# Reordering the load queue behind the context loop of a perceiver block

## Chip, cores, metric

One core of one Trainium2 chip. The metric is the device time in microseconds of one execution of the whole kernel, as the median of several runs. The profiled execution is one more run.

## What is computed

`x` is 256 x 2048, the context 25088 x 2048. Cut to what matters:

```python
def reference(x, ctx, Wq, bq, Wk, bk, Wv, bv, W_base, b_base, W_gate, A, B):
    x = x + cross_attention(layernorm(x), ctx)        # softmax(q @ ctx.T) @ ctx, no projections
    h = layernorm(x)                                  # 32 heads of 64, 8 of them for k and v
    q = einsum('bse,edh->bsdh', h, Wq) + bq           # Wq is summed over groups of 4 heads first
    k = einsum('bse,edh->bsdh', h, Wk) + bk
    v = einsum('bse,edh->bsdh', h, Wv) + bv
    # for each token: scores over the 64 x 64 pairs of head *elements*, softmax, times v
    x = x + attention_within_token(q, k, v)
    h = layernorm(x)
    result = h @ W_base.T + b_base
    probs = softmax(h @ W_gate.T); top-2 of 8 experts, renormalised -> route_w
    delta = einsum(einsum(h, A) * route_w, B)         # LoRA experts of rank 16
    return x + result + delta
```

## The kernel before, in words

The kernel is written engine by engine, and each engine runs its own list in order; semaphores tie them together. The order of the loads is the order in which the SP list issues them. Every float32 product is made of three float32r products, of a high half (`nat_hi`, `xt_hi`) and a low half (`nat_lo`, `xt_lo`), the latter being the difference to the former (L1004 to L1006).

**The loop.** 49 blocks of 512 context rows. A block comes twice: as quarters (`quart`, L330), which VectorE transposes into chunks for the scores, and as rows in four pieces of 1 MB (`raw`, L323), which ScalarE casts to `nat_hi` (`hi_piece`, L557) and GpSimd subtracts to `nat_lo` (`lo_piece`, L475). `raw` holds two pieces: piece j + 2 can be loaded once piece j has been split, which is what `nat_ready[j]` counts. Wq's sum over head groups is made in the loop and stored to `wq_dram`.

**Behind the loop** three weights are read in the same four pieces, in the order Wk, Wq (from `wq_dram`), Wv. SP's list before: two pieces of Wk; bk and bv (L398); eight loads of LoRA's B into `b_nat` (L401), each 16 x 128 rows of 64 B; four loads of the gate into `side_rows` and four of LoRA's A into `a_nat` (L338), rows of 128 B; then the other ten pieces in a list `order` with the waits on `nat_ready`. Within the list stand `store_qk(0, 1)` (L415), which stores k to DRAM in three bfloat16 parts when VectorE has counted `qk_split`, and `heads_back(1, k_t, ...)` (L423), twelve loads that bring the parts back with tokens along the free axis; each has eight rows of 16 KB. Behind the list come q's store and q's twelve loads into `q_t`, then `b_base_all` (L438), and, when TensorE has done the gate (`G_GATE`), the second half of the first block of W_base (L330). `b_nat` and `side_rows` lie in the buffer that this half takes.

**ScalarE** casts Wk piece 0, makes `std` of the first tile of tokens (L540), casts piece 1, drains that tile's transposes into `xt_hi`, casts pieces 2 and 3, and then makes `std` of the second tile. **GpSimd** splits Wk, **VectorE** splits Wq and Wv (L881) and the parts of q and k (L887, L893).

**TensorE** multiplies the first tile of 128 tokens by all of Wk, transposes the second tile, multiplies that one; then Wq for both, then Wv for both, with the bias as a product ahead of each (L1120). Then it waits for `b_loaded` and `a_loaded`, transposes B and A in groups of four (L1034, L1013) and the gate (L1155), waits for `qk_back`, and starts the attention scores (`pair_scores`, L1165). Attention, the third layer norm, the router and the base product follow. The lines in its list around this place:

```python
            pe.wait_ge(b_loaded, 16 * EXPERTS)
            pe.wait_ge(a_loaded, 16 * QR)
            ...
            pe.wait_ge(qk_back, 16 * TT * (len(Q_PARTS) + len(K_PARTS)))
            ...
            for o in range(2):
                pair_scores(o)
```

Of the kernel before, what the change touches and what calls it, by code (L numbers as in the profile page):

```python
# [14 lines left out]
P = 128  # L15
# [13 lines left out]
def perceiver_block(nc, x, ctx, wq, bq, wk, bk, wv, bv, w_base, b_base, w_gate, lora_a, lora_b, out):  # L29
# [9 lines left out]


    _, TOK, DIM = x.shape
    KEYS = ctx.shape[1]
    DH, HEADS = bq.shape
    KVH = bk.shape[1]
    REP = HEADS // KVH
    EXPERTS, RANK, _ = lora_a.shape
    OUTF = w_base.shape[0]
    TT = TOK // P
    DC = DIM // P
    KB = 512  # L50
    KT = KB // P
    NB = KEYS // KB
# [8 lines left out]
    QR = P // SQ  # L61
# [24 lines left out]
    with ExitStack() as stack:  # L86
        def sem(name):
            return stack.enter_context(nc.semaphore(name))
# [10 lines left out]
        def put(at, name, shape, dt=F32):  # L99
            return nc.alloc_sbuf_tensor_at(name, shape, dt, offset=at)  # L100
# [21 lines left out]
        a_nat = put(at_tr, "a_nat", [P, DIM])  # L122
# [22 lines left out]
        k_t = put(at_probs, "k_t", [P, P, DH], BF16)  # L145
        x_hat2 = put(at_probs, "x_hat2", [P, TT, DIM])
        side_rows = put(at_quart + 16 * KIB, "side_rows", [P, DIM])
        b_nat = put(at_quart + 24 * KIB, "b_nat", [P, DC, ER])
# [76 lines left out]
        chunk_split = sem("chunk_split")  # L225
# [25 lines left out]
        a_loaded = sem("a_loaded")  # L251
        b_loaded = sem("b_loaded")
        gate_loaded = sem("gate_loaded")
# [67 lines left out]
        def _(sp):  # L321
            def load_rows(j, src):
                sp.dma_start(raw[:, j % 2], src).then_inc(raw_loaded[j], 16)  # L323
# [12 lines left out]
            def load_in_chunks(to, src, a, done):  # L336

                sp.dma_start(to.rearrange("p (c a i) -> p a c i", a=QR, i=SQ)[:, a],  # L338
                             src[:, a * QF:(a + 1) * QF].rearrange("p (c i) -> p c i", i=SQ)).then_inc(done, 16)
# [57 lines left out]
            for col, b_ in enumerate((bk, bv)):  # L397
                sp.dma_start(side_rows[0:1, col * QKC:(col + 1) * QKC],  # L398
                             b_.rearrange("(a d) h -> a (d h)", a=1)).then_inc(bias_loaded, 16)
            for e in range(EXPERTS):  # L400
                sp.dma_start(b_nat[:, :, e * RANK:(e + 1) * RANK],  # L401
                             lora_b[e].rearrange("(o p) r -> p o r", p=P)).then_inc(b_loaded, 16)
            for a in range(QR):
                load_in_chunks(side_rows[64:64 + EXPERTS, :], w_gate, a, gate_loaded)
            sp.wait_ge(chunk_split, DC * NB)
            for a in range(QR):
                load_in_chunks(a_nat[:], lora_a.rearrange("e r d -> (e r) d"), a, a_loaded)
            sp.wait_ge(wq_stored, 16 * DC)


# [1 line left out]
            def store_qk(n, w):  # L412
                for t in range(TT):
                    sp.wait_ge(qk_split, TT * n + t + 1)
                    sp.dma_start(qk_dram[w, :, :, t * P:(t + 1) * P].rearrange("s g m d -> m (s g) d"),  # L415
                                 qk_nat[:, w, t].rearrange("p s (g d) -> p (s g) d", d=DH)).then_inc(qk_stored, 16)

            def heads_back(w, to, parts):
                sp.wait_ge(qk_stored, TT * (2 - w) * 16)
                for k, part in enumerate(parts):  # L420
                    for t in range(TT):
                        at = P // TT * t + KVH * k
                        sp.dma_start(to[at:at + KVH], qk_dram[w, part, :, t * P:(t + 1) * P]).then_inc(qk_back, 16)  # L423

            order = [(n, src, j) for n, src in enumerate((wk_rows, wq_rows, wv_rows)) for j in range(PIECES)]
            for n, src, j in order[2:]:
                if (n, j) == (2, 1):
                    store_qk(0, 1)
                if (n, j) == (2, 2):
                    heads_back(1, k_t, K_PARTS)  # L430
                sp.wait_ge(nat_ready[(j + 2) % 4], NB + n + (j >= 2))
                load_rows(j, src[:, 4 * j:4 * j + 4, :])
            store_qk(1, 0)
            for j in range(PIECES):
                sp.wait_ge(nat_ready[j], NB + 3)
            heads_back(0, q_t, Q_PARTS)
            sp.wait_ge(qkv_done, 3 * TT)
            sp.dma_start(b_base_all[:], b_base.unsqueeze(0).broadcast_to([P, OUTF])).then_inc(bias_loaded, 16)  # L438

# [800 lines left out]
K_PARTS = (0, 1, 0, 1, 2, 0)  # L1240
# [24 lines left out]
```

## Time and profile before

| | us |
|---|---|
| median of 3 runs | 2553.24 |
| lowest, highest | 2550.48, 2562.08 |
| profiled execution | 2560.45 |
| its span from first to last instruction | 2558.6 |
| TensorE busy in the span | 2458.9 (96%) |
| VectorE busy | 1975.5 (77%) |
| GpSimd busy | 1265.1 (49%) |
| ScalarE busy | 1081.6 (42%) |

All times of instructions below are counted from the start of the span. A line such as `start us, us, engine line op out<-in xcount [idle before <-releaser]` tells when an instruction began, how long it took, and, in brackets, how long the engine had been idle before it and whose event ended that. For a transfer the time is that of the issue on the SP queue; the time to its landing stands in the DMA view. The loop ends near 2198 us; the stretch that the change touches reaches from there to the start of attention.

### The profile page before, as it was taken

How to read it: one execution, taken by the hardware profiler on the slowest of the kernel's cores; microseconds unless marked ns; L12 is line 12 of the kernel's file. 1: busy time of each engine (PE TensorE's matmuls, PEld its weight loads, DVE VectorE, ACT ScalarE, POOL GpSimd, SP SyncE). 2: the span in 40 equal slices, each digit the busy share in tenths (PEclk: the TensorE clock that was granted, in tenths of full speed). 3: DMA queues.
4: the chain of work that ended last, by engine and by line, in shares of the span. 5: the costliest groups of instructions: out<-in, count | busy, mean ns of one | idle time of the engine just before them, and what ended most of it. 6: DMA issues, size and time to landing. Idle time of an engine off the chain costs nothing.

```text
span 2558.6 us, 35034 instructions
## 1 busy us (share of the span) xinstructions
PE 2458.9 (96%) x11342; PEld 2025.2 (79%) x11342; DVE 1975.5 (77%) x2668; ACT 1081.6 (42%) x1547; POOL 1265.1 (49%) x896
## 2 busy tenths in 40 slices
PE   6999999999999999999999999999999999894799
PEld 4888888888888888888888888888888888763677
DVE  7788888888888888888888887787878778532668
ACT  4444444444444444444444444444444444222323
POOL 4455556565556556655665565555555555410000
PEclk9999999999999999999999999999999999996579
DMA  9787887788788778878887877787777777667046
GB/s 243 200 217 182 215 202 195 200 209 212 194 206 213 195 196 209 206 197 213 201 204 194 210 190 189 191 196 184 192 184 186 188 188 192 166 138 113 5 85 145
DMA packets 377515, 476.14 MB, mean 186 GB/s; under 512 B 48707, under 2 KB 265795, under 8 KB 374853
## 3 DMA queue, kind: packets, MB, share of 16 engines
q1 hardware_dynamic: 373894, 454.68, 73.3%
q0 software_dynamic: 3584, 20.97, 2.6%
q8 instruction: 23, 0.38, 0.1%
q14 instruction: 14, 0.11, 0.0%
HBM read 467.74 MB, written 7.86 MB: 186 GB/s over the span
## 4 chain that ended last, share of the span: by engine, by line
PE 89%; DMA 4%; DVE 3%; SPq 2%; ACT 1%; POOL 1%; issue 1%; DVEq 0%; ACTq 0%
PE ps L1004 28%; PE ps L1006 28%; PE ps L1005 28%; PE ps L1013 2%; DMA raw<-in_L_attn_Wv_dram 1%; DMA q_t<-qk_dram 1%; DVE ch_lo L768 1%; PE ps L1034 1%; SPq L330 1%; DMA raw<-in_ctx_dram 1%; POOL nat_lo L475 1%; PE ps L1197 1%; DVE tr L764 1%; ACT nat_hi L557 1%; PE ps L1165 0%
## 5 line engine op out<-in xcount | busy, mean ns | idle before, releaser
L475 POOL TENSOR_TENSOR nat_lo<-raw,nat_hi 128x512 fp32r<-128x512 f32 x800 | 1172.8, 1496 | 933.3 <-ACT nat_hi L557 931.0
L768 DVE TENSOR_TENSOR ch_lo<-tr,ch_hi 128x512 fp32r<-128x512 f32 x848 | 949.9, 1120 | 362.6 <-ACT ch_hi L534 360.7
L534 ACT CAST ch_hi<-tr 128x512 fp32r<-128x512 f32 x848 | 517.2, 621 | 876.2 <-PE ps L1006 857.1
L1004 PE MATMUL ps<-ch_hi,xt_hi 128*128 128x512 f32 x1696 | 674.5, 398 | 8.1 <-DVE ch_lo L768 7.7
L1006 PE MATMUL ps<-ch_hi,xt_lo 128*128 128x512 f32 x1696 | 663.5, 391 | 0.0
L1005 PE MATMUL ps<-ch_lo,xt_hi 128*128 128x512 f32 x1696 | 662.9, 391 | 0.0
L1004 PE MATMUL ps<-nat_hi,pt_hi 128*128 128x512 f32 x1568 | 610.3, 389 | 2.9 <-DVE pt_lo L698 2.9
L1006 PE MATMUL ps<-nat_hi,pt_lo 128*128 128x512 f32 x1568 | 610.2, 389 | 0.0
L1005 PE MATMUL ps<-nat_lo,pt_hi 128*128 128x512 f32 x1568 | 610.0, 389 | 0.0
L764 DVE STREAM_TRANSPOSE tr<-quart 128x512 f32<-128x512 f32 x848 | 592.8, 699 | 3.9 <-DMA quart<-in_L_ffn_W_base_dram 3.8
L557 ACT CAST nat_hi<-raw 128x2048 fp32r<-128x2048 f32 x208 | 397.5, 1911 | 276.9 <-PE ps L1006 215.3
L1004 PEld LDWEIGHTS ps<-ch_hi,xt_hi 128*128 128x128 f32 x1696 | 320.0, 189 | 77.5 <-DVE ch_lo L768 9.1
L1006 PEld LDWEIGHTS ps<-ch_hi,xt_lo 128*128 128x128 f32 x1696 | 319.7, 189 | 68.4
L1005 PEld LDWEIGHTS ps<-ch_lo,xt_hi 128*128 128x128 f32 x1696 | 320.0, 189 | 64.4 <-issue 0.8
L1004 PEld LDWEIGHTS ps<-nat_hi,pt_hi 128*128 128x128 f32 x1568 | 294.3, 188 | 65.3 <-DVE pt_lo L698 4.0
L1005 PEld LDWEIGHTS ps<-nat_lo,pt_hi 128*128 128x128 f32 x1568 | 294.3, 188 | 61.3
L1006 PEld LDWEIGHTS ps<-nat_hi,pt_lo 128*128 128x128 f32 x1568 | 294.3, 188 | 61.2
L806 DVE SCALAR_TENSOR_TENSOR acc<-acc,alpha,ps 128x512 f32<-128x512 f32 x248 | 177.6, 717 | 41.9 <-PE ps L1006 40.2
L518 ACT CAST pt_hi<-ps 128x512 fp32r<-128x512 f32 x98 | 57.2, 584 | 120.8 <-PE ps L1013 120.8
L815 DVE SCALAR_TENSOR_TENSOR acc<-acc,alpha,ps 128x512 f32<-128x512 f32 x144 | 101.2, 703 | 4.9 <-PE ps L1006 4.9
L563 ACT ACTIVATE probs<-ps,neg_max 128x512 f32<-128x512 f32 x98 | 66.9, 683 | 67.4 <-DVE neg_max L788 67.4
L785 DVE TENSOR_REDUCE blk_max<-ps 128x1 f32<-128x512 f32 x98 | 65.5, 668 | 6.8 <-PE ps L1006 6.8
(126 smaller groups left out, 941.7 us busy)
## 6 DMA issues: line engine op xcount, KB each, us to landing
quart<-in_ctx_dram SPq DMA_DIRECT2D x392, 512.0 KB, 8.3
raw<-in_ctx_dram SPq DMA_DIRECT2D x196, 1024.0 KB, 7.8
wq_in<-in_L_attn_Wq_dram POOLq DMA_DIRECT2D x16, 1024.0 KB, 11.9
quart<-in_L_ffn_W_base_dram SPq DMA_DIRECT2D x32, 512.0 KB, 8.6
wq_dram<-wq_out POOLq DMA_DIRECT2D x16, 256.0 KB, 2.3
raw<-in_L_attn_Wk_dram SPq DMA_DIRECT2D x4, 1024.0 KB, 6.3
raw<-wq_dram SPq DMA_DIRECT2D x4, 1024.0 KB, 5.2
raw<-in_L_attn_Wv_dram SPq DMA_DIRECT2D x4, 1024.0 KB, 17.6
```

The source lines that it names most:

```text
L475: last = pool.tensor_tensor(nat_lo[:, j, t], raw[:, j % 2, t], nat_hi[:, j, t].bitcast(F32), ALU.subtract)
L534: act.copy(ch_hi[:, c % RING_CH, :], tr[:, c % RING_TR, :]).then_inc(chunk_hi, 1)
L557: act.copy(nat_hi[:, j], raw[:, j % 2]).then_inc(nat_hi_ready, 1)
L563: act.activation(probs[:, q, :], ps[:, SCORE_BANK + TT * new + q, :], ACT.Exp, bias=neg_max[:, new, q:q + 1], accum_out=row_sum[:, q:q + 1 ...
L764: dve.transpose(tr[:, c % RING_TR, :].rearrange("p (r i) -> p r i", i=SQ), src).then_inc(chunk_transposed, 1)
L768: dve.tensor_tensor(ch_lo[:, c % RING_CH, :], tr[:, c % RING_TR, :], ch_hi[:, c % RING_CH, :].bitcast(F32), ALU.subtract).then_inc(chunk_s ...
L785: dve.tensor_reduce(blk_max[:, q:q + 1], ps[:, SCORE_BANK + TT * new + q, :], AX.X, ALU.max, negate=True).then_inc(blkmax_ready, 1)
L806: dve.scalar_tensor_tensor(piece, piece, alpha[:, 1 - turn.parity, q:q + 1], ps[:, out_bank(v, turn.over), :], ALU.mult, ALU.add).then_inc ...
L815: dve.scalar_tensor_tensor(piece, piece, alpha[:, turn.parity, q:q + 1], ps[:, out_bank(v, False), :], ALU.mult, ALU.add).then_inc(acc_upd ...
L1004: pe.matmul(out_, a_hi, b_hi, start=start, stop=False)
L1005: pe.matmul(out_, a_hi, b_lo, start=False, stop=False)
L1006: return pe.matmul(out_, a_lo, b_hi, start=False, stop=stop)
```

## The change

SP's list behind the loop is put in another order. No transfer is added, removed or changed in shape, and no other engine's list is touched.
- The eight B loads, the four gate loads and the four A loads (with the wait on `chunk_split` ahead of the latter) go from behind bk and bv to behind q's way back, ahead of the wait for `qkv_done` and of `b_base_all`.
- The ten other pieces of Wk, Wq and Wv follow bk and bv at once.
- k's store goes from ahead of Wv's second piece to behind Wq's last, ahead of Wv's first. k's way back is now written behind the load of Wv's second piece, where before it was written ahead of the wait for Wv's third.

```diff
             for col, b_ in enumerate((bk, bv)):
                 sp.dma_start(side_rows[...], b_...).then_inc(bias_loaded, 16)
+            sp.wait_ge(wq_stored, 16 * DC)
...
+            order = [(n, src, j) for n, src in enumerate((wk_rows, wq_rows, wv_rows)) for j in range(PIECES)]
+            for n, src, j in order[2:]:
+                sp.wait_ge(nat_ready[(j + 2) % 4], NB + n + (j >= 2))
+                load_rows(j, src[:, 4 * j:4 * j + 4, :])
+                if (n, j) == (1, 3):
+                    store_qk(0, 1)
+                if (n, j) == (2, 1):
+                    heads_back(1, k_t, K_PARTS)
+            store_qk(1, 0)
+            for j in range(PIECES):
+                sp.wait_ge(nat_ready[j], NB + 3)
+            heads_back(0, q_t, Q_PARTS)
             for e in range(EXPERTS):
                 sp.dma_start(b_nat[...], lora_b[e]...).then_inc(b_loaded, 16)
             for a in range(QR):
                 load_in_chunks(side_rows[64:64 + EXPERTS, :], w_gate, a, gate_loaded)
             sp.wait_ge(chunk_split, DC * NB)
             for a in range(QR):
                 load_in_chunks(a_nat[:], lora_a..., a, a_loaded)
-            sp.wait_ge(wq_stored, 16 * DC)
...
-            for n, src, j in order[2:]:
-                if (n, j) == (2, 1):
-                    store_qk(0, 1)
-                if (n, j) == (2, 2):
-                    heads_back(1, k_t, K_PARTS)
-                sp.wait_ge(nat_ready[(j + 2) % 4], NB + n + (j >= 2))
-                load_rows(j, src[:, 4 * j:4 * j + 4, :])
-            store_qk(1, 0)
-            for j in range(PIECES):
-                sp.wait_ge(nat_ready[j], NB + 3)
-            heads_back(0, q_t, Q_PARTS)
             sp.wait_ge(qkv_done, 3 * TT)
             sp.dma_start(b_base_all[:], ...).then_inc(bias_loaded, 16)
```

## Rows read from the trace of the kernel before

**Rows 1.** The page, its first line.

```profile
span 2558.6 us, 35034 instructions
```

**Rows 2.** TensorE's waits, 2228 to 2370 us: who waited for whom, sum, times, longest.

```profile
PE ps L1004 <- DVE nat_lo L881: 17.0, 1, 17.0
PE ps L1165 <- DMA q_t<-qk_dram: 16.2, 1, 16.2
PE ps L1004 <- POOL nat_lo L475: 8.7, 2, 8.2
```

**Rows 3.** The chain that ended last, 2050 to 2560 us: start, us, what.

```profile
2293.14 26.55 DMA raw<-in_L_attn_Wv_dram
...
2336.00 21.52 DMA q_t<-qk_dram
...
2426.91 6.17 PE ps L1013 x28
```

**Rows 4.** Timeline of the SP queue: start, time over which issued, line, transfer, count.

```profile
2199.96 7.17 SPq L323 DMA_DIRECT2D raw<-in_L_attn_Wk_dram  x2
...
2207.88 12.75 SPq L401 DMA_DIRECT2D b_nat<-in_L_ffn_B_dram  x8
...
2222.70 6.75 SPq L338 DMA_DIRECT2D a_nat<-in_L_ffn_A_dram  x4
2229.56 2.26 SPq L323 DMA_DIRECT2D raw<-in_L_attn_Wk_dram  x2
...
2272.74 0.37 SPq L323 DMA_DIRECT2D raw<-in_L_attn_Wv_dram  x1
2277.98 2.17 SPq L415 DMA_DIRECT2D qk_dram<-qk_nat  x2
2280.19 1.86 SPq L323 DMA_DIRECT2D raw<-in_L_attn_Wv_dram  x1
2284.43 4.01 SPq L423 DMA_DIRECT2D k_t<-qk_dram  x12
2288.49 5.05 SPq L323 DMA_DIRECT2D raw<-in_L_attn_Wv_dram  x2
...
2332.01 4.29 SPq L423 DMA_DIRECT2D q_t<-qk_dram  x12
```

**Rows 5.** Timeline of GpSimd, 2190 to 2330 us.

```profile
2216.70 10.94 POOL L475 TENSOR_TENSOR nat_lo<-raw,nat_hi 128x512 fp32r<-128x512 f32 x8 [9.96 <-ACT nat_hi L557]
2238.46 10.85 POOL L475 TENSOR_TENSOR nat_lo<-raw,nat_hi 128x512 fp32r<-128x512 f32 x8 [10.82 <-ACT nat_hi L557]
```

**Rows 6.** DMA view, issues in 2200 to 2207 us: count, KB, us to landing.

```profile
raw<-in_L_attn_Wk_dram SPq DMA_DIRECT2D x2, 1024.0 KB, 5.7
```

**Rows 7.** Timeline of ScalarE, 2235 to 2242 us.

```profile
2236.48 1.90 ACT L557 CAST nat_hi<-raw 128x2048 fp32r<-128x2048 f32 x1 [10.53 <-DMA raw<-in_L_attn_Wk_dram]
```

**Rows 8.** DMA view, 2223 to 2233.2 us: packets, and a pair of loads.

```profile
DMA packets 8586, 1.24 MB, mean 122 GB/s; under 512 B 8514, under 2 KB 8514, under 8 KB 8585
...
raw<-in_L_attn_Wk_dram SPq DMA_DIRECT2D x2, 1024.0 KB, 7.4
```

**Rows 9.** DMA view, 2314.2 to 2319 us: packets, MB, share of 16 engines.

```profile
q1 hardware_dynamic: 474, 0.94, 50.6%
```

**Rows 10.** DMA view, issues in 2284 to 2290 us.

```profile
raw<-in_L_attn_Wv_dram SPq DMA_DIRECT2D x1, 1024.0 KB, 28.7
```

**Rows 11.** Tile b_nat: count, ns min/median/max, first and last start.

```profile
L1034 PE MATMUL ps<-ident,b_nat x16: 272/273/332, 2335.1 to 2338.9; 128*128 128x128 f32 x16
```

**Rows 12.** Windows: busy time by engine, granted TensorE clock, DMA share, GB/s.

```profile
2334.00:2342.00 8.00, 6.33 (x54) 5.28 (x52) 4.32 (x7) 5.35 (x11) 2.68 (x3) 1.00 0.81 107
2426.00:2434.00 8.00, 6.59 (x32) 6.35 (x32) 6.54 (x9) 4.42 (x8) 0.00 (x0) 0.57 0.00 0
```

**Rows 13.** DMA view, 2211 to 2223 us: packets.

```profile
DMA packets 16906, 1.27 MB, mean 106 GB/s; under 512 B 16816, under 2 KB 16816, under 8 KB 16906
```

**Rows 14.** Line 330, 2340 to 2359 us: count, ns min/median/max, first and last start.

```profile
L330 SPq DMA_DIRECT2D quart<-in_L_ffn_W_base_dram x4: 334/3493/9389, 2341.5 to 2351.8; - x4
```

More of the change, by code:

```diff
@@ L399, in _ @@
                              b_.rearrange("(a d) h -> a (d h)", a=1)).then_inc(bias_loaded, 16)
[L400 to L407, printed above, removed]
             sp.wait_ge(wq_stored, 16 * DC)
@@ L436, in _ @@
             heads_back(0, q_t, Q_PARTS)
+            for e in range(EXPERTS):
+                sp.dma_start(b_nat[:, :, e * RANK:(e + 1) * RANK],
+                             lora_b[e].rearrange("(o p) r -> p o r", p=P)).then_inc(b_loaded, 16)
+            for a in range(QR):
+                load_in_chunks(side_rows[64:64 + EXPERTS, :], w_gate, a, gate_loaded)
+            sp.wait_ge(chunk_split, DC * NB)
+            for a in range(QR):
+                load_in_chunks(a_nat[:], lora_a.rearrange("e r d -> (e r) d"), a, a_loaded)
             sp.wait_ge(qkv_done, 3 * TT)
```

## Prediction

> **What bounds the kernel now.** I read the page first: its span is 2558.6 us, and the profiled execution took 2560.45 us, against a median of 2553.24 us [rows 1]. Nearly all of it is the loop over the context, in which nothing changes. So I work only on the stretch behind the loop, from 2199.96 us on, when the rows of Wk begin to load, to 2357.5 us, when attention begins. I read the stretch as a chain of waits. TensorE's own waits there are three: 8.7 us for the low halves of Wk that GpSimd makes, 17.0 us for the low halves of Wv, and 16.2 us for q_t on its way back from DRAM [rows 2]. The chain names the two late ends of these: the last Wv load, with 26.55 us from its issue, and q_t, with 21.52 us from its last issue [rows 3]. The reader should see that this stretch hangs on the SP queue and on the transfers behind it, and that from 2357.5 us on everything follows from the start of the attention scores: a step that moves this start moves the end by as much.
>
> **Wk, third and fourth piece: what is removed from ahead of them.** Before, SP issues bk and bv, then eight loads of b_nat (12.75 us), four of the gate and four of a_nat (6.75 us), and only then, at 2229.56 us, the third piece of Wk [rows 4]. What it has to wait for is `nat_ready[0]`, GpSimd's split of piece 0. GpSimd does pieces 0 and 1 as eight instructions from 2216.70 us in 10.94 us [rows 5], so piece 0 is done after half of that, at 2222.2, and piece 1 at 2227.6. In the changed kernel SP stands at exactly these waits. A Wk load that ran with nothing beside it landed 5.7 us after its issue [rows 6]: the third piece lands at 2227.9, the fourth at 2233.4. ScalarE cast the third at 2236.48 [rows 7] and takes 1.9 us, so now the casts end at 2229.8 and 2235.3. GpSimd follows with 5.4 us for each and ends at 2240.8, where it ended at 2238.46 + 10.85 = 2249.3 [rows 5]. That is **8.5 us earlier**. If the loads land in 7.4 us, as a pair did beside other traffic [rows 8], it is 6.8. ScalarE's `std` of the second tile of tokens is queued behind the fourth cast and comes early with it. TensorE has its other half of the first tile done by then, and the second tile, then Wq, follow without a new wait. Wq's loads wait for the same kind of event (GpSimd's splits of Wk, VectorE's of Wq) and move along. I take 8.5.
>
> **Key store one place earlier.** I count this on the old clock, before the shift of 8.5. The old order was first Wv piece at 2272.74, store of k at 2277.98 (2.17 us of issue, with its wait for `qk_split`), second Wv piece at 2280.19, k_t back at 2284.43, third and fourth Wv piece at 2288.49 and up to 2293.5 [rows 4]. Queued behind the store's wait is now the first Wv piece: it is issued near 2280.2 instead of 2272.74. Who needs it is TensorE at the end of Wq. 1 MB of such rows moves in about 2.7 us once it runs: 0.94 MB took the 4.8 us from 2314.2 us on at a share of 50.6% of the engines [rows 9], so 2.4 us of all of them; with issue and landing it is the 5.7 us of [rows 6]. The store's rows end near 2283, so the first piece lands at 2287.5 and its split ends at 2291.7. TensorE had Wq done at 2291.4: it costs nothing, by a margin near nought, with cover if it is late of only the 17.0 us wait for the third piece [rows 2]. What does cost is that k_t now queues behind two Wv pieces, not one. It starts 2.7 us later, and the third and fourth Wv piece land behind it: the third took 28.7 us to land beside k_t [rows 10], and it is its landing that TensorE's 17.0 us wait is for. So 2.7 us of the 8.5 go back. Bounds are 0, if k_t starts as before, and 4: k_t's transfers end near 2314 [rows 9], 29.5 us after their first issue [rows 4], where q_t took 25.5, so that much is what other loads beside such a transfer can cost. The k_t issues themselves keep their place between the second and third piece. **Net 5.8 us earlier** for everything up to q_t's store and its way back: its first issue goes from 2332.01 [rows 4] to 2326.2.
>
> **LoRA and gate rows last: what is added behind q_t.** TensorE's program doesn't change: after Wv it waits for `b_loaded` and `a_loaded`, makes 32 transposes and the 16 small ones of the gate, and only then waits for `qk_back` and starts the scores. Before, all of it was done by 2357.5 - 16.2 = 2341.3, in the shadow of q_t. It began near 2335.1 [rows 11], so it took 6.2 us, at a granted clock of 1.00, the 2.4 GHz level [rows 12]. Now the small loads are issued behind q_t's twelve. Two questions decide the price: how long they take, and whether they run beside q_t.
> How long: b_nat, gate and a_nat are 16384 rows of 64 B and 8704 of 128 B. In 2211 to 2233.2 us lie 16816 + 8514 = 25330 packets under 512 B, which are all of them (the few more are those that count a transfer as landed), so 22.2 us at most [rows 8, 13]. I take 21.7, with 21 as the lower end, as SP was held on the second b_nat load till about 2212. Rows count here, not bytes: 2 MB of long rows would move in 5.4 us by the rate above.
> Beside q_t or not: the third Wv piece, issued right behind k_t's last, landed after 28.7 us instead of 5.7 [rows 6, 10]. And of four W_base loads issued behind q_t from 2341.49 on, one held SP for 9.39 us [rows 14]. Each says that what is issued behind twelve such transfers gets through after them, and that SP is held when it issues more. So the small loads take their 21.7 us from q_t's end on. q_t's end is 2357.5 - 2332.0 = 25.5 us after its first issue [rows 3, 4]. I take 1.5 off the sum of the two, as part of the first b_nat load is through by then, and b_base, which ran beside q_t, now comes last.
> The Trainium skill ("DMA: Bandwidth & Descriptors", section "Bandwidth") gives 6.15 us for a load of 1 MB; by it b_nat and a_nat would be an estimated 12.3 us, and the sum some 9 us less. Its loads are of long rows; the trace here shows 22.2 us for 64 and 128 B rows [rows 8, 13].
> TensorE then has idled for some 40 us. During x_hat's transposes, which came behind a wait too, the granted clock was 0.57 on the mean, near the 1.2 GHz level [rows 12]. There 28 of them took 6.17 us, 0.22 us each [rows 3]. So 32 take 7.0 us, the gate's about 2, together **9 us**, all on the path where it had been hidden. If the clock stayed up it would be 6.2.
>
> **Sum.** -5.8 + 21.7 - 1.5 + 9 = +23.4, which I round to +23 us. Attention starts at 2380.5 instead of 2357.5. Behind it b_base and the W_base loads come 23 us later too, but they are needed in x2 and in the second half of the first output block, some 60 and 100 us later. No load is added or removed. On the profiled execution 2560.45 becomes 2583.5; on the median 2553.24 becomes 2576. By the smaller ends of each step (-8.5 + 21 - 4 + 6.2; the 4 is q_t's time beside no other load at all) it is +15, by the larger (-(6.8 - 4) + 22.2 + 9.3) +29: the likeliest case's own range is 2568 to 2582.
>
> **The rivals.**
> **Small loads run beside q_t.** Had SP not been held, the last a_nat is issued 4.3 + 12.75 + 2.0 + 6.75 = 25.8 us after q_t's first issue, lands 5.7 later, and with 9 us of transposes the scores start 40.5 us after 2326.2, at 2366.7: +9, 2562 us. For it: q_t's transfers have eight rows each and load only part of the DMA engines, since in 2314.2 to 2319 us, after k_t, the share was 50.6% while the rest of Wv drained [rows 9]. Against it: that same stretch shows the other part still waiting its turn, and each small load needs all parts. The Trainium skill (same page, "Why a DMA increments its semaphore by 16 and not by 1") has a DMA of eight rows on the eight lowest-numbered of 16 engines, and the trace agrees with the 50.6%; by it the free half helps only half of each small load.
> **Small loads overtake q_t, and it gets faster.** If rows of 64 B pass between q_t's long rows, and a_nat has landed by 16.5 us after q_t's first issue, the transposes end in q_t's shadow and only the gain is left: -5.8, 2547 us. That is the point from which it decides. Against it: the issue alone takes 25.8 us, whatever the transfers do, so it needs an issue that is faster than on [rows 4].
> **It costs more.** The gain shrinks to 2 us since the k store's new place costs TensorE a wait at Wv, and q_t is 4 us slower beside small rows, as k_t was beside Wv: -2 + 4 + 21.7 + 9 = +33, 2586 us. For it: the margin of the first Wv piece is near nought.
>
> **How the numbers follow.** Forecast 0.70, small loads beside q_t 0.13, overtaking 0.05, dearer 0.12. 0.5% is 12.8 us, about what can be told from no change. Forecast and dearer are slower by more: 0.82, and with the upper end of the second case 0.83. Within 0.5%: 0.12. Faster by more than 0.5% only by overtaking at its best, which at -5.8 is itself within 0.5%: of its 0.05 I put 0.02 on faster and 0.03 on the same, so 0.15 the same. The range reaches from 2562, the case beside q_t, to 2585, near the dearer one.
>
> **What would show it.** Third and fourth Wk load issued near 2222 and 2228, GpSimd's last split ending near 2241; q_t's first issue near 2326; one of the first small issues held for over 10 us; a wait of TensorE of about 40 us that ends on a_nat or b_nat, then the transposes at a clock near 0.5, then scores with no wait for q_t. I am wrong if TensorE waits for q_t still, or if the small loads end less than 35 us after q_t's first issue.

## The result, and the profile after

| | median us | runs | range |
|---|---|---|---|
| before | 2553.69 | 8 | 2550.48 to 2562.44 |
| after | 2572.78 | 8 | 2566.65 to 2580.89 |

The ratio is 1.0067, with a 95% interval of 1.0045 to 1.0090: the changed kernel is slower by 17 to 19 us. The profiled execution took 2572.55 us. The ratios of the experiments below are to the runs of the kernel before that were taken beside them, with medians of 2556.83 us (e1 to e4) and 2554.24 us (e5 to e8).

The page of the changed kernel, its first line, which answers [rows 1]:

```profile
span 2570.8 us, 35034 instructions
```

TensorE's waits from 2228 to 2420 us in the changed kernel (who waited for whom, sum, times, longest), which answer [rows 2]:

```profile
PE ps L1034 <- DMA a_nat<-in_L_ffn_A_dram: 42.5, 1, 42.5
PE ps L1004 <- DVE nat_lo L881: 16.5, 1, 16.5
...
PE ps L1004 <- POOL nat_lo L475: 2.9, 1, 2.9
```

The wait for GpSimd's low halves of Wk shrank from 8.7 to 2.9 us. The one for Wv is what it was. The 16.2 us for q_t are gone, and in their place stands a wait of 42.5 us for a_nat. Nothing waits for q_t any more: it has long landed.

The SP queue (start, time over which issued, line, transfer, count), which answers [rows 4]:

```profile
2202.56 7.17 SPq L323 DMA_DIRECT2D raw<-in_L_attn_Wk_dram  x2
...
2224.41 6.26 SPq L323 DMA_DIRECT2D raw<-in_L_attn_Wk_dram  x2
...
2273.92 2.16 SPq L407 DMA_DIRECT2D qk_dram<-qk_nat  x2
2276.12 2.42 SPq L323 DMA_DIRECT2D raw<-in_L_attn_Wv_dram  x2
2280.87 4.16 SPq L415 DMA_DIRECT2D k_t<-qk_dram  x12
2288.32 4.93 SPq L323 DMA_DIRECT2D raw<-in_L_attn_Wv_dram  x2
...
2327.43 4.00 SPq L415 DMA_DIRECT2D q_t<-qk_dram  x12
2331.47 29.51 SPq L430 DMA_DIRECT2D b_nat<-in_L_ffn_B_dram  x8
...
2363.56 5.68 SPq L338 DMA_DIRECT2D a_nat<-in_L_ffn_A_dram  x4
```

The third and fourth Wk piece go out 21.9 us after the first, where it was 29.6. And the eight b_nat loads, which took 12.75 us to issue ahead of Wk, take 29.51 us behind q_t. The chain of the changed kernel shows where (start, us, what), which answers [rows 3]:

```profile
2331.91 21.54 SPq L430
2353.49 1.44 SPq L430
...
2367.82 5.14 DMA a_nat<-in_L_ffn_A_dram
2373.09 1.09 PE ps L1034 x4
...
2379.36 1.12 PE ps L1155 x16
2380.48 0.82 PE ps L1165 x32
```

The second b_nat issue alone is held for 21.54 us, until q_t's rows are through. What the DMA engines moved meanwhile shows in the DMA view, of 2332 to 2334 us and of 2334 to 2352 us:

```profile
DMA packets 1048, 0.20 MB, mean 98 GB/s; under 512 B 1040, under 2 KB 1040, under 8 KB 1040
```

```profile
q1 hardware_dynamic: 128, 1.05, 47.0%
```

Of the 2048 rows of the first b_nat load, 1024 went in the first 2 us. In the 18 us after them the trace has 64 packets of 16 KB, which are q_t's rows, and no row of b_nat; about half of the 16 engines are busy. All of q_t is 96 such packets, of 2.07 us each (median). Eight of them are under way at a time for 23.3 us, and the last ends at 2352.85 us. So half of the engines are free, but half of the first load is left to the engines that q_t keeps busy. Then come the other loads at their usual pace, and a_nat lands; TensorE makes its transposes, and at 2380.48 the scores start. GpSimd's low halves of Wk, which answer [rows 5]:

```profile
2219.29 10.96 POOL L475 TENSOR_TENSOR nat_lo<-raw,nat_hi 128x512 fp32r<-128x512 f32 x8 [9.95 <-ACT nat_hi L557]
2231.40 12.12 POOL L475 TENSOR_TENSOR nat_lo<-raw,nat_hi 128x512 fp32r<-128x512 f32 x8 [1.15 <-ACT nat_hi L557]
```

The loop itself ended 2.6 us later in this execution (Wk's first load at 2202.56 and not 2199.96). From here on, times in a table count from Wk's first load, so that this does not enter.

| us after Wk's first load | before | before, again | after | after, again |
|---|---|---|---|---|
| GpSimd's last split ends | 49.3 | 47.9 | 41.0 | 41.0 |
| k's store issued | 78.0 | 78.2 | 71.4 | 71.3 |
| q_t's first load issued | 132.1 | 131.9 | 124.9 | 125.0 |
| b_nat's first transpose | 135.1 | 135.1 | 170.5 | 169.1 |
| scores start | 157.6 | 158.8 | 177.9 | 175.9 |
| x_hat's first transpose | 227.0 | 228.1 | 246.3 | 244.4 |
| end | 358.6 | 357.6 | 368.2 | 375.5 |

The columns "again" are second profiles of the same two kernels, taken as e9 and e10 below. Attention starts 18.7 us later on the mean of two. The last row shows something else: from x_hat's first transpose to the end it is 131.7, 129.5, 121.9 and 131.1 us, and that has nothing to do with the change (e9 and e10).

### The profile page after: what moved, and what is told of

Its sections match the earlier page's. It is cut to its first block, busy times and chain, and to the rows that moved or that the text cites. A ratio compares the mean times of both kernels' runs of the same rounds, so it can differ in the third digit from the quotient of the medians.

```text
span 2570.8 us, 35034 instructions
## 1 busy us (share of the span) xinstructions
PE 2445.0 (95%) x11342; PEld 2012.1 (78%) x11342; DVE 1976.1 (77%) x2668; ACT 1080.5 (42%) x1547; POOL 1268.5 (49%) x896
## 4 chain that ended last, share of the span: by engine, by line
PE 89%; DVE 3%; DMA 3%; SPq 2%; ACT 1%; POOL 1%; issue 1%; ACTq 0%; DVEq 0%
PE ps L1004 28%; PE ps L1006 28%; PE ps L1005 28%; PE ps L1013 2%; DMA raw<-in_L_attn_Wv_dram 1%; SPq L430 1%; DVE ch_lo L768 1%; PE ps L1034 1%; POOL nat_lo L475 1%; SPq L330 1%; DVE tr L764 1%; DMA raw<-in_ctx_dram 1%; PE ps L1197 1%; ACT nat_hi L557 1%; PE ps L1165 0%
```

## The experiments

My theory after the result: the transposes of B and A had been hidden in TensorE's wait for q_t; now their loads stand behind q_t, so that TensorE waits for them instead. The gain at Wk is real and smaller. Open were three things: whether k's store has a share, why the small loads wait for q_t (the order of SP's queue, or the DMA engines), and what each small load costs.

### e1: the small loads last, k's store at its old place

```diff
-                if (n, j) == (1, 3):
+                if (n, j) == (2, 0):
                     store_qk(0, 1)
```

> The changed kernel with k's store back at its old place, ahead of Wv's second piece; the small loads stay last. Theory (the small loads carry the whole loss, the store's place is worth nothing): attention starts within 2 us of the changed kernel's once the loop's end is taken off, the time is within 3 us of its 2573 us. Rival (the store's new place costs the 2.7 us of the prediction, as k_t queues behind two Wv pieces): q_t's first issue is 2.7 us earlier against the end of Wk's splits than in the changed kernel. The wait of TensorE for a_nat is 42 to 43 us by both.

Measured: 2571.82 us (2569.81 to 2574.96, 5 runs), ratio to before 1.0059 [1.0038, 1.0079]. Its SP queue, first Wk and q_t loads:

```profile
2201.73 7.17 SPq L323 DMA_DIRECT2D raw<-in_L_attn_Wk_dram  x2
...
2327.32 4.00 SPq L415 DMA_DIRECT2D q_t<-qk_dram  x12
```

q_t's first issue is 125.6 us after Wk's first load, 0.7 us later than in the changed kernel and not 2.7 earlier; the wait for a_nat is 41.6 us. As far as these runs can tell, the small loads' place carries the whole loss, and k's store shows no share in it.

### e2 and e11: k's store alone

```diff
-                if (n, j) == (2, 1):
-                    store_qk(0, 1)
...
+                if (n, j) == (1, 3):
+                    store_qk(0, 1)
```

> The kernel before with k's store one place earlier and nothing else; the small loads stand ahead of Wk's third piece again. Theory: no change that can be told, 2552 to 2556 us; Wk's splits end 49 to 50 us after Wk's first load is issued, as before, and TensorE waits some 16 us for q_t. Rival (the earlier store delays k_t and by it Wv's last pieces): q_t's first issue 2.7 us later than before, 2557 us.

Measured: 2554.84 us (11 runs), ratio 1.0004 [0.9989, 1.0020]. In time no difference can be told (the interval reaches from 3 us less to 5 us more). But its profile did not fit: q_t's first issue came 136.2 us after Wk's first load, 4 us later than before.

The SP queue of e2, first Wk and q_t loads:

```profile
2200.95 7.18 SPq L323 DMA_DIRECT2D raw<-in_L_attn_Wk_dram  x2
...
2337.11 4.29 SPq L423 DMA_DIRECT2D q_t<-qk_dram  x12
```

A second profile of the same kernel, e11, was to tell spread from cost:

> The kernel of e2_store_only, profiled once more: there q_t's first issue came 4.1 us later after Wk's first load than in before (136.2 against 132.1), in part since k's store itself came 1.9 us later. Theory (that is the spread of k_t's stretch from execution to execution): 131 to 135 us here. Rival (the store's place costs it): 136 us again.

The same two rows of e11's SP queue:

```profile
2200.47 7.19 SPq L323 DMA_DIRECT2D raw<-in_L_attn_Wk_dram  x2
...
2332.79 4.29 SPq L423 DMA_DIRECT2D q_t<-qk_dram  x12
```

132.3 us, as before. TensorE was late already at k's store in e2 (80.0 us after Wk's first load against 78.1 here). The rest lies in the stretch from k's store to q_t's first issue, and that differs much from execution to execution: with the store at its new place it took 53.5 and 53.7 us (after, e10), 49.5 (e3), 55.4 (e4), 55.2 (e6), 56.2 (e2) and 54.3 (e11), at the old place 54.0, 53.7 (before, e9) and 52.9 us (e1). On the means that is 0.4 us more. The store's place costs nothing that can be told, but a cost of 1 or 2 us could hide in such a spread.

### e3: the small loads on a queue of their own

They are taken out of SP's list and stand in ScalarE's, behind the copies of v_dup.

```diff
-            for e in range(EXPERTS):
-                sp.dma_start(b_nat[...], lora_b[e]...).then_inc(b_loaded, 16)
...
+            act.wait_ge(qk_stored, 4 * 16)
+            act.wait_ge(chunk_transposed, DC * NB)
+            for e in range(EXPERTS):
+                act.dma_start(b_nat[...], lora_b[e]...).then_inc(b_loaded, 16)
...
+            act.wait_ge(chunk_split, DC * NB)
+            for a in range(QR):
+                act_in_chunks(a_nat[:], lora_a..., a, a_loaded)
```

> The changed kernel, but the sixteen small loads are issued by ScalarE's queue in place of SP's, at the same time: behind a wait for q's store and the two v_dup copies, so some 4 us after q_t's first issue. Theory (on SP's queue the second small load stands behind q_t's long rows, because one queue is served in its order): on a queue of their own the small rows go beside q_t, no issue is held for 21 us, and TensorE's wait for a_nat falls from 42.5 us to 20 to 28 us; the time is 2551 to 2560 us. Rival (it is the DMA engines that are busy with q_t, not the queue that is in order): the wait for a_nat stays at 40 to 46 us, the time at 2570 to 2580.

Measured: 2573.58 us (6 runs), ratio 1.0075 [1.0050, 1.0099]. My theory fell. The chain:

```profile
2324.05 21.88 ACTq L639
2345.96 4.33 ACTq L639
```

TensorE's waits in the same kernel:

```profile
PE ps L1041 <- DMA a_nat<-in_L_ffn_A_dram: 45.2, 1, 45.2
```

ScalarE's queue issues its first b_nat load 2.4 us after q_t's first, has the second held for 22.4 us (21.88 of them in the chain), just as SP had, and TensorE waits 45.2 us. (From q_t's first issue to the first transpose it is 47.5 us, against 45.7 and 44.0 in the changed kernel.) The small loads do not wait because they share a queue with q_t. The DMA view of 2328 to 2346 us shows what ScalarE's queue got through:

```profile
q1 hardware_dynamic: 206, 1.56, 71.4%
q10 hardware_dynamic: 104, 0.01, 1.2%
```

Its own queue did let small rows in between q_t's: 104 rows of 64 B, beside 64 rows of 16 KB, where SP's queue had let none. But that is one or two small rows for each long one, and the rest of the load waited. What is left is the DMA engines: each small load has a share on all of them, and those that carry q_t's long rows come to it last. e5 puts that to the test.

### e4: the small loads in gaps of the queue

The edit is shown against the changed kernel; the lines at the small loads' place behind q_t go.

```diff
+            for e in range(EXPERTS):
+                sp.dma_start(b_nat[...], lora_b[e]...).then_inc(b_loaded, 16)
             sp.wait_ge(wq_stored, 16 * DC)
...
+                if (n, j) == (1, 1):
+                    for a in range(QR):
+                        load_in_chunks(side_rows[64:64 + EXPERTS, :], w_gate, a, gate_loaded)
+                    sp.wait_ge(chunk_split, DC * NB)
+                    for a in range(QR):
+                        load_in_chunks(a_nat[:], lora_a..., a, a_loaded)
```

> The changed kernel with no small load last: the eight b_nat loads stand ahead of Wk's third piece, as in the kernel before, the four gate and four a_nat loads behind Wq's second piece, where SP and the DMA engines rest. Theory (the gain of 7 us comes from the a_nat loads that held Wk's third piece back; b_nat alone ends before that piece may be issued): GpSimd's last split ends 8 us earlier than before, attention starts 6 to 8 us earlier than before, the transposes of b_nat and a_nat lie in q_t's shadow again; 2545 to 2549 us. Rival (what is gained at Wk is given back at Wv or to TensorE's clock): attention starts within 3 us of before, 2551 to 2556 us.

Measured: 2553.13 us (2539.51 to 2557.85, 12 runs), ratio 0.9980 [0.9963, 0.9997]. GpSimd's splits of Wk:

```profile
2218.81 10.96 POOL L476 TENSOR_TENSOR nat_lo<-raw,nat_hi 128x512 fp32r<-128x512 f32 x8 [9.95 <-ACT nat_hi L558]
2230.93 12.24 POOL L476 TENSOR_TENSOR nat_lo<-raw,nat_hi 128x512 fp32r<-128x512 f32 x8 [1.15 <-ACT nat_hi L558]
```

TensorE's waits in e4, for q_t and for Wv:

```profile
PE ps L1166 <- DMA q_t<-qk_dram: 17.6, 1, 17.6
PE ps L1005 <- DVE nat_lo L882: 16.8, 1, 16.8
```

The last split ends 41.1 us after Wk's first load, 8.2 less than before, and attention starts at 151.7 and not 157.6. So the gain of some 6 us is there to be had in the profile, and it is the gate and a_nat loads, not b_nat's, that held Wk's third piece. The time missed its expected range (2545 to 2549 us) and lies in the rival's: the median is 3.7 us below the runs of before, where 6 to 8 were expected. The interval of the ratio, 1 to 9 us less, holds both numbers, so the timed runs do not say how much of the 6 us arrives.

### e5: fewer long rows on the busy engines

```diff
-Q_PARTS = (0, 0, 1, 1, 0, 2)
-K_PARTS = (0, 1, 0, 1, 2, 0)
+Q_PARTS = (0, 1, 0, 0, 1, 2)
+K_PARTS = (0, 1, 1, 2, 0, 0)
...
+                        if two:
+                            sp.dma_start(to[at:at + 2 * KVH], qk_dram[w, parts[k]:parts[k] + 2, :, t * P:(t + 1) * P]
+                                         .rearrange("s g m d -> (s g) m d")).then_inc(qk_back, 16)
...
```

> The changed kernel, with the way back of k and q in loads of up to 16 rows of 16 KB: the slots are put in the order q 0,1,0,0,1,2 and k 0,1,1,2,0,0 (the same six products), so that four of six slots of a tile are loaded two at a time: 8 loads in place of 12 for each of k and q. Theory (the DMA engines that carry the 8-row loads are the bound of q_t's stretch, two us for each 16 KB row, and the small rows wait for those engines, whatever their queue): those engines have 8 rows each and not 12, so the hold of the second b_nat issue falls from 21.5 us to 13 to 15, TensorE's wait for a_nat from 42.5 to 34 to 36, and k_t's stretch by 6 to 8 more: 2556 to 2562 us. Rival (the 16 KB rows are bound by DRAM or by a limit that all engines share): the hold stays at 20 to 22 us and the time at 2568 to 2575.

Measured: 2556.74 us (2555.07 to 2562.45, 12 runs), ratio 1.0005 [0.9992, 1.0019]: this alone takes back what the change had lost. The second b_nat issue in its chain:

```profile
2322.71 13.82 SPq L437
```

TensorE's waits in e5:

```profile
PE ps L1041 <- DMA a_nat<-in_L_ffn_A_dram: 33.7, 1, 33.7
```

The hold falls from 21.54 us (19.98 in e10, 20.64 in e1) to 13.82, by about a third, where the engines that have most of q_t's rows have 8 of them and not 12, a third less. From q_t's first issue to the end of the hold it is 26.0 us for 12 rows and 17.3 us for 8: 2.2 us for a row in both. The number of loads falls by a third as well, so a price for each load would give the same. The trace decides between the two: the packets of 16 KB take 2.05 us each (median) as they did, and now up to 16 of them are under way at a time, for 6.8 us, and eight for 6.7. It is the rows on the busiest engines that set the time, and the rival's limit shared by all engines is out. Not all of the 16 us by which e5 beats the changed kernel is the hold. q_t's first issue also comes 5.8 us earlier than there; but in e3, with the old loads, it came as early, so one profile does not show that k_t's new loads are the reason. The Trainium skill ("DMA: Bandwidth & Descriptors", section "Why a DMA increments its semaphore by 16 and not by 1") says that a DMA from these queues runs on as many of the 16 engines as divides its outermost count, on the lowest-numbered ones: 8 for 8 rows, 16 for 16. The trace agrees: eight packets of 16 KB at a time with loads of 8 rows, up to 16 with those of 16 rows. By it engine 0 carries 12 rows of q_t before and 8 now.

### e6: only gate and a_nat last

```diff
+            for e in range(EXPERTS):
+                sp.dma_start(b_nat[...], lora_b[e]...).then_inc(b_loaded, 16)
             sp.wait_ge(wq_stored, 16 * DC)
...
             heads_back(0, q_t, Q_PARTS)
-            for e in range(EXPERTS):
-                sp.dma_start(b_nat[...], lora_b[e]...).then_inc(b_loaded, 16)
```

> The changed kernel with the eight b_nat loads back ahead of Wk's third piece, so that only the gate and a_nat loads stand last. Theory (each small load costs its own time behind q_t): the early gain stays, since b_nat's issues end before Wk's third piece may be issued, and of the 21 us behind q_t the 11.5 of b_nat go: attention starts 10 to 12 us earlier than in the changed kernel, 2561 to 2564 us. Rival (b_nat is what held Wk back): GpSimd's last split ends over 3 us later than in the changed kernel, 2565 or more.

Measured: 2559.48 us (2555.01 to 2568.04, 10 runs), ratio 1.0018 [1.0000, 1.0036].

TensorE's waits in e6, for comparison with the 42.5 us of the changed kernel:

```profile
PE ps L1034 <- DMA a_nat<-in_L_ffn_A_dram: 30.7, 1, 30.7
```

The time is 1.5 us under the expected range. TensorE's wait falls from 42.5 to 30.7 us, and attention starts at 166.7 us after Wk's first load, 11.2 less than in the first profile of the changed kernel and 9.3 less than in the second; the last split ends at 41.0, so b_nat had not held Wk. The two kinds of small loads each cost their own time behind q_t.

### e7 and e8: k's way back behind Wv

Both start from e4, since it showed the wait for Wv untouched at 16.8 us.

```diff
-                if (n, j) == (2, 1):
+                if (n, j) == (2, 3):
                     heads_back(1, k_t, K_PARTS)
```

> The kernel of e4_split_places with k's way back issued behind Wv's fourth piece and not ahead of its third. Theory (TensorE's 17 us wait at Wv is for pieces that stand behind k_t's 16 KB rows): this wait falls under 3 us, q's store goes 13 to 16 us earlier; but q_t's rows then stand behind k_t's on the same engines, 24 and 24 us after one another, from some 92 us after Wk's first load: attention starts near 141 us after it, where it was 151.7; 2538 to 2544 us. Rival (the rows of Wv are slowed by something else): the wait at Wv stays above 10 us, 2550 to 2556.

Measured: 2544.46 us (2535.56 to 2553.53, 12 runs), ratio 0.9963 [0.9946, 0.9980]. TensorE's 17 us wait for Wv is gone. But the time is 0.5 us over the expected range, and attention starts at 145.6 us after Wk's first load, not 141. The SP queue:

```profile
2290.84 5.23 SPq L418 DMA_DIRECT2D k_t<-qk_dram  x12
2305.90 9.84 SPq L410 DMA_DIRECT2D qk_dram<-qk_nat  x2
2319.99 4.29 SPq L418 DMA_DIRECT2D q_t<-qk_dram  x12
```

TensorE's waits in e7:

```profile
PE ps L1166 <- DMA q_t<-qk_dram: 30.7, 1, 30.7
```

q's store now stands behind k_t's rows too, which I had not counted: its two issues take 9.84 us and q_t is issued 14.1 us after the store, where it was 6.1 us.

e8 puts e5's loads of 16 rows into e7:

> As e7_split_k_late, with the loads of up to 16 rows of e5_after_16rows. Theory: k_t and q_t take 16 us each on the engines they load most, not 24, so attention starts near 126 us after Wk's first load; 2523 to 2530 us. Rival (16 KB rows share a limit): no more than 3 us less than e7_split_k_late.

Measured: **2529.33 us** (2526.86 to 2535.57, 6 runs), ratio 0.9902 [0.9881, 0.9922]. It beats the kernel before by 1.0%, and the changed kernel by more.

TensorE's waits in e8, for q_t and for Wv:

```profile
PE ps L1173 <- DMA q_t<-qk_dram: 14.3, 1, 14.3
...
PE ps L1012 <- DVE nat_lo L889: 3.4, 1, 3.4
```

Attention starts at 135.7 us after Wk's first load. It was to be 126: the time came out in the range expected, but the step to it did not, so the hit does not support that step. Wv's last cast began at 102.3 us and not at 97.0 as in e7, and q's store was issued at 108.6; why the fourth Wv piece is later here is open. The wait for q_t is 14.3 us, less than half of e7's.

### e9 and e10: the two kernels profiled again

> The kernel before, profiled once more, to see what of the difference between the two first profiles belongs to the execution and not to the kernel. Theory (the 9.7 us by which the stretch from x_hat's first transpose to the end was longer in the profile of before, 131.7 against 122.0 us, came from TensorE's granted clock in the router products of that one execution): here it is 122 to 123 us, with the clock back at 1.00 by the router's products, while attention starts 157 to 160 us after Wk's first load as before. Rival (it is a property of the kernel before): 130 us or more again.

> The changed kernel, profiled once more. Theory: the early part repeats to 1 us (GpSimd's last split 41 us after Wk's first load), TensorE's wait for a_nat to 2 us (42.5), attention starts 176 to 180 us after Wk's first load; k_t's and q_t's stretches may each differ by 2 us. Rival (the loss hangs on a state of the DMA engines): attention starts outside 174 to 182 us.

They took 2560.85 and 2578.19 us, one execution each. e10 came as expected: the last split ends at 41.0 us, TensorE waits 42.1 us for a_nat, and attention starts at the edge of the range. The windows behind that, in x_hat's transposes and the router's products, each beginning 8 to 12 us after x_hat's first transpose (span, busy of the five engines, granted clock, DMA share, GB/s), first of before:

```profile
2436.00:2456.00 20.00, 20.00 (x94) 19.71 (x94) 3.94 (x5) 0.61 (x4) 0.00 (x0) 0.51 0.00 1
```

before again:

```profile
2438.00:2458.00 20.00, 20.00 (x94) 19.95 (x94) 4.05 (x3) 0.00 (x0) 0.00 (x0) 0.50 0.00 1
```

after:

```profile
2460.90:2472.90 12.00, 12.00 (x82) 10.99 (x82) 4.68 (x23) 2.67 (x8) 0.00 (x0) 1.00 0.00 0
```

after again:

```profile
2455.00:2475.00 20.00, 20.00 (x90) 19.61 (x91) 3.94 (x11) 0.61 (x4) 0.00 (x0) 0.50 0.00 0
```

e9 missed its expectation: the kernel before was slow there twice, 129.5 us where I had expected 122. But the changed kernel was slow there in one of its two, and e2 and e11, whose code from attention on is the same, had 122.3 and 121.9. So it goes with the execution and with the granted clock: 0.50 or 0.51, the 1.2 GHz level, against 1.00. It is worth 8 to 10 us. Of the 13 profiles only these three were slow there, among them both of the kernel before; with so few, whether that kernel falls into it more often stays open, as does what decides it.

## Why the prediction was right, point by point

The median came out at 2572.8 us, 3 us under the 2576 of the forecast and inside its likeliest case (2568 to 2582). The case was the forecast one. Its three terms, however, were each off by 1 to 2 us, all towards a larger loss: 1.2 us too little gain, 1.6 us too much for the small loads and 1.9 us too much for the transposes.

**Wk, 8.5 us earlier.** Right: GpSimd's last split ended 8.4 us earlier in the first pair of profiles and 6.9 in the second, as the kernel before had it at 49.3 and at 47.9 us. The loads landed 5.0 us after issue.

**TensorE follows without a new wait.** Right, but for TensorE's clock. At k's store 6.7 of the 8.4 us were left in the first pair of profiles, and 6.8 of the 6.9 in the second. In the first profile of the changed kernel the second half of the first tile's products ran in part at the 1.2 GHz level, 0.63 us for each and not 0.39:

```profile
2243.57 0.53 PE L1004 MATMUL ps<-nat_hi,xt_hi 128*128 128x512 f32 x1 [2.89 <-POOL nat_lo L475]
...
2245.18 0.63 PE L1005 MATMUL ps<-nat_lo,xt_hi 128*128 128x512 f32 x1
```

In the first profile of the kernel before, the granted clock was back at 1.00 for them (window of before from 2250 us on, columns as in [rows 12]):

```profile
2250.00:2252.00 2.00, 2.00 (x11) 1.63 (x10) 0.00 (x0) 0.00 (x0) 0.00 (x0) 1.00 0.59 144
```

From the last split's end to k's store it is 28.7 us there and 30.4 in the changed kernel. But the change is not the reason: the kernel before had 30.3 us in its second profile, with the clock low for a while further on, and e3 and e4, which have the gain at Wk too, had 28.7 and 28.8, with the clock at 1.00 throughout. So 1.7 us come and go with the clock, in both kernels. What decides it, no run isolates.

**k's store, 2.7 us lost.** Mis-sized: nothing of it can be told. From k's store to q_t's first issue it is 54.0 and 53.7 us before, 53.5 and 53.7 after, 52.9 in e1, with the spread that e2 has shown. The step "k_t starts later, and all behind it is as much later" shows in neither pair of profiles. The landings of Wv's four pieces (min, median, max) suggest why, before and after:

```profile
DMA to landing us min/median/max: 5.0/17.6/28.7
```

```profile
DMA to landing us min/median/max: 7.9/16.4/24.2
```

The longest landing, of the third piece, fell from 28.7 to 24.2 us: k_t did stand behind two pieces, but the third piece was issued later beside it, and the stretch that both share ended at the same point. My reading, which e1 with the old order agrees with but no run isolates: Wv and k_t are one sum of work for the same DMA engines, and its order inside does not move its end. The first Wv piece, issued late as foreseen, was in time: TensorE has no second wait for Wv.

**Net 5.8 us for q_t's first issue.** It was 7.2 and 6.8: too much gain at Wk and too much loss at Wv, which cancel in part, by luck.

**Small loads behind q_t, 45.7 us after its first issue.** 25.5 + 21.7 - 1.5 = 45.7; measured 45.7 and 44.0. That SP is held was right too: 21.54 us on one issue. The reading behind it, that what is issued later gets through later, holds on SP's queue, and the DMA view of 2334 to 2352 us shows it. Across queues it holds but for a few rows (104 of them in 18 us, e3). The prediction's doubt that the free half of the engines helps was right too: it took its half of the first load at once, and nothing more. e6 sizes the parts: 9 to 11 us for b_nat by the start of attention, 11 to 13 by the time from q_t's first issue to the first transpose (32.9 us in e6), the rest for gate and a_nat.

The figure of the Trainium skill ("DMA: Bandwidth & Descriptors", section "Bandwidth"), 6.15 us for 1 MB in a load issued from GpSimd, by which this term would have been an estimated 9 us less, does not hold for such rows: b_nat alone, 1 MB in rows of 64 B, cost 9 to 13 us (e6).

**Transposes, 9 us.** 7.4 and 6.9: mis-sized by 1.6 to 2.1 us. TensorE began them at the low level, as assumed, but did not stay there:

```profile
2364.00:2376.00 12.00, 2.91 (x14) 2.94 (x15) 0.31 (x1) 1.25 (x3) 0.00 (x0) 0.50 0.77 176
2377.00:2381.00 4.00, 3.44 (x59) 3.08 (x58) 2.26 (x4) 2.68 (x6) 0.00 (x0) 1.00 0.01 4
```

In the first window, four transposes took 0.85 us and more; in the second the clock was at the 2.4 GHz level.

**The rivals.** Small loads beside q_t: out, by the hold of 21.54 us and by e3. Overtaking: out, as no row of b_nat went between q_t's from 2334 to 2352 us. Dearer: out, as the store's place cost nothing that can be told and q_t was not slower beside small rows (its last row ended 25.4 us after its first issue, where 25.5 were counted). The sum of the measured terms is -7.0 + (44.8 - 26.2) + 7.1 = +18.7 us on the means of two profiles (26.2 being q_t's first issue to the scores before), 0.9 less by the time of x_hat, and +17 to +19 by the runs.

## What to carry to other kernels

A load that is moved out of the way must be priced where it lands: who consumes it, in what shadow that work had been, and which long transfer now stands ahead of it. Transfers of a few long rows, which load only some of the DMA engines, are the ones to keep out of the way of others, or to issue with more rows at a time; a second queue does not get round them. Where two transfers feed one wait, put the one whose consumer comes first ahead (e7), and shrink the other (e8).

## What the runs showed of the hardware that I had not expected

- A DMA issue on ScalarE's queue was held 22.4 us behind transfers of SP's queue, as long as on SP's own (21.5 us). In 18 us of it 104 rows of 64 B passed between 64 rows of 16 KB; on SP's own queue none did.
- A row of 16 KB took 2.07 us on its engine (median of q_t's 96 in the changed kernel), 8 GB/s, with eight under way at a time, and 2.05 us with up to 16.
- 12 loads of 8 rows of 16 KB held the small loads for 21.5 us; the same bytes in 8 loads, half of them of 16 rows, for 13.8 us.
- The granted clock in the stretch of the router's products was 0.50 or 1.00 in executions of one and the same kernel, 9 us apart.
